# Attention: each pair's V products moved next to the scores that follow them, and the output projection moved into the banks of the q, k, v products

## What is computed

```python
h = _ln(x, ln1_g, ln1_b) + shift
qkv = (h @ Wqkv.T).reshape(b, n, 3, H, HD)
q = _ln(qkv[:, :, 0].transpose(0, 2, 1, 3), qn_g, qn_b)
k = _ln(qkv[:, :, 1].transpose(0, 2, 1, 3), kn_g, kn_b)
v = qkv[:, :, 2].transpose(0, 2, 1, 3)
scores = jnp.einsum('bhnd,bhmd->bhnm', q, k) / jnp.sqrt(jnp.float32(HD))
attn = jax.nn.softmax(scores, axis=-1)
o = jnp.einsum('bhnm,bhmd->bhnd', attn, v)
o = o.transpose(0, 2, 1, 3).reshape(b, n, H * HD)
x = x + o @ Wout.T
gate = jax.nn.softmax(tok @ Wgate.T, axis=-1)
```

## Time and profile before

| | |
|---|---|
| times of three runs | 1450.46, 1447.7, 1451.57 us |
| median | 1450.46 us |
| span of the profiled execution, first to last instruction | 1449.0 us |
| TensorE matmuls busy | 1391.5 us, 96% |
| TensorE weight loads | 1175.2 us, 81% |
| ScalarE | 1041.2 us, 72% |
| VectorE | 968.6 us, 67% |
| GpSimd | 913.1 us, 63% |
| mean granted TensorE clock | 0.986 of 2.4 GHz |

### The profile page before, as it was taken

One profiled execution on the slowest core, in us unless ns is written; L12 is line 12 of the kernel. 1 busy time (PEld: TensorE's weight loads), 2 busy tenths in 40 slices (PEclk: granted clock), 3 DMA queues, 4 the chain that ended last, 5 costly groups with the idle time before them and its releaser, 6 DMA issues. The chain is left out here.

```text
span 1449.0 us, 30428 instructions
## 1 busy us (share of the span) xinstructions
PE 1391.5 (96%) x10795; PEld 1175.2 (81%) x10795; DVE 968.6 (67%) x2250; ACT 1041.2 (72%) x2762; POOL 913.1 (63%) x855
## 2 busy tenths in 40 slices
PE   7899999997899999999999999999999989999997
PEld 6899999995677877787787778777787778889896
DVE  6877776645666676576667667667656568678763
ACT  5566666556898789888888888888988742466662
POOL 2676667643668767867776876876777620364633
PEclk9899999999999999999999999999999999999999
DMA  5432222110100100110110110011011127145522
GB/s 157 130 109 67 73 67 74 48 30 30 37 9 30 52 34 19 53 45 9 52 45 17 44 52 23 31 52 45 9 45 38 37 99 296 37 107 152 140 34 29
DMA packets 61638, 89.04 MB, mean 61 GB/s; under 512 B 6144, under 2 KB 50992, under 8 KB 58800
## 3 DMA queue, kind: packets, MB, share of 16 engines
q1 hardware_dynamic: 53232, 75.82, 16.1%
q0 software_dynamic: 6144, 8.39, 3.5%
q10 hardware_dynamic: 2112, 2.88, 0.6%
HBM read 61.90 MB, written 25.18 MB: 60 GB/s over the span
## 5 line engine op out<-in xcount | busy, mean ns | idle before, releaser
L1349 POOL TENSOR_TENSOR prob<-prob,share_p 128x512 f32<-128x512 f32 x256 | 271.8, 1069 | 214.3 <-DVE share_p L1456 214.3
L1450 DVE TENSOR_REDUCE shift<-bank 128x2 f32<-128x512 f32 x256 | 164.7, 684 | 235.2 <-PE bank L1083 235.2
L1230 ACT ACTIVATE prob<-bank,shift 128x256 f32<-128x256 f32 x512 | 236.8, 485 | 77.7 <-DVE shift L1450 77.6
L147 PE MATMUL bank<-wqkv_h,rowsT_h 128*128 128x512 f32 x384 | 159.5, 415 | 2.8 <-PEq L311 1.7
L147 PE MATMUL bank<-wqkv_h,rowsT_l 128*128 128x512 f32 x384 | 151.1, 394 | 0.0
L147 PE MATMUL bank<-wqkv_l,rowsT_h 128*128 128x512 f32 x384 | 151.0, 393 | 0.0
L1110 PE MATMUL bank<-pT,landing 128*64 128x256 f32 x1024 | 139.6, 394 | 4.4 <-ACT pT L1306 4.4
L1095 PE MATMUL bank<-ident,prob 128*128 128x128 f32 x1024 | 140.3, 280 | 0.5 <-POOL prob L1349 0.5
L1337 POOL TENSOR_TENSOR landing<-landing,rq 128x512 f32<-128x512 f32 x128 | 132.0, 1053 | 8.4 <-DVE rq L1404 8.4
L1095 PEld LDWEIGHTS bank<-ident,prob 128*128 128x128 f32 x1024 | 109.5, 141 | 18.6 <-POOL prob L1349 1.0
L1230 ACT ACTIVATION_READ_ACCUMULATOR prob<-bank,shift 128x1 f32 x512 | 110.9, 217 | 0.0
(11 more groups left out here) (324 smaller groups left out, 4557.4 us busy)
## 6 DMA issues: line engine op xcount, KB each, us to landing
landing<-in_fc1s SPq DMA_DIRECT2D x6, 1024.0 KB, 4.8
landing<-in_fc2s SPq DMA_DIRECT2D x6, 1024.0 KB, 4.8
rows<-in_x SPq DMA_DIRECT2D x16, 256.0 KB, 3.0
xT<-in_xT SPq DMA_DIRECT2D x16, 256.0 KB, 2.7
x_again<-in_x SPq DMA_DIRECT2D x16, 256.0 KB, 2.7
x_rows<-x SPq DMA_DIRECT2D x16, 256.0 KB, 3.2
rows<-x_rows SPq DMA_DIRECT2D x16, 256.0 KB, 3.1
x<-x_rows SPq DMA_DIRECT2D x16, 256.0 KB, 2.8
```

The lines of the kernel that those rows point to most:

```text
L147: last = nc.tensor.matmul(out, a, b, start=(n == 0), stop=(n == 3 * len(ks) - 1))
L1230: last = nc.scalar.activation(prob[at][:, n, :], score_bank[side][:, n * T:(n + 1) * T], ACT.Exp, bias=shift[:, at, n:n + 1], scale=-1.0, ...
L1349: nc.gpsimd.tensor_tensor(prob[at][:, :, :], prob[at][:, :, :], share[:, at, :].unsqueeze(2).to_broadcast([P, TT, T]), ALU.mult).then_inc( ...
L1450: nc.vector.tensor_reduce(shift[:, s % 2 * 2 + side, :], score_bank[side][:, :].rearrange("p (n m) -> p n m", n=TT), AX, ALU.min).then_inc ...
```

## The change

On TensorE the odd fill moves from behind the V products to before them, in all blocks but the closing one. So the order of a pair step becomes scores, transposes, even fill, chunks or projection, odd fill, V products, and the next pair's scores follow the V products directly. The projection of sequences 0 to 13 writes the chunk banks instead of `tr`; its two entries leave `TR_FILLS`, and it waits for the chunk that used the bank before (`chunk_out`), while chunks 8 and 9 wait for its copy (`out_proj`). For sequences 14 and 15 it stays where it was. On ScalarE, at the start of a pair step, the copy of the projection and the emptying of the odd fill now come before the taking of the V products; the copy of the projection thereby moves from the end of pairs 2 and 3 to the start of pairs 3 and 4. Where the even fill is emptied does not change.

```diff
-TR_FILLS = [("x2", 0, 1), ("h", 0, 2), ("gates", 0, 3), ("proj", 0, 4), ("qk", 0, 5), ("proj", 1, 6)] + [("qk", j, 6 + j) for j in range(1, 8)]
+TR_FILLS = [("x2", 0, 1), ("h", 0, 2), ("gates", 0, 3), ("qk", 0, 5)] + [("qk", j, 6 + j) for j in range(1, 8)]
+PROJ_PAIRS = 2, 3
...
+        def proj_bank(b, n):
+            return chunk_bank[n] if b < NB - 2 else tr
...
-                def project(t, b, n, its):
+                def project(b, n, its):
                     wait(pe, o_lo, PAIRS, b, PAIRS)
+                    if b < NB - 2:
+                        wait(pe, chunk_out, 12, b + 2, 7 + n)
+                    else:
+                        wait(pe, out_gates, 1, b - 1, 1)
+                        wait(pe, out_proj, TT, b, n)
...
-                    tr_free(pe, t, "proj", n)
-                    product(nc, tr[:, 0:D], ...
+                    product(nc, proj_bank(b, n)[:, 0:D], ...
...
                     wait(pe, chunk_out, 12, b, j - 1)
+                    if j in (8, 9):
+                        wait(pe, out_proj, TT, b - 2, j - 7)
...
                         for c, j in chunks_at(t, s):
                             if live(c):
                                 chunk(c, j)
-                        c, name, n = fill_at(t, 2 * s)
-                        if name == "proj" and live(c) and not closing(t):
-                            project(t, c, n, 1 - odd)
+                        if not closing(t):
+                            if s in PROJ_PAIRS and live(t - 1):
+                                project(t - 1, PROJ_PAIRS.index(s), 1 - odd)
+                            fill(t, 2 * s + 1)
                         for b, q, its in values_at(t, s, odd):
                             if live(b):
                                 values(b, q, its)
...
-                        fill(t, 2 * s + 1)
+                        if closing(t):
+                            fill(t, 2 * s + 1)
...
                     for s in range(PAIRS):
+                        if not closing(t) and not closing(t - 1):
+                            if s - 1 in PROJ_PAIRS and live(t - 1):
+                                projected(t - 1, PROJ_PAIRS.index(s - 1))
+                            empty(*fill_at(t, 2 * s - 1), 1 - odd)
                         for b, q, its in taken_at(t, s, odd):
...
-                        empty(*fill_at(t, 2 * s - 1), 1 - odd)
+                        if closing(t) or closing(t - 1):
+                            empty(*fill_at(t, 2 * s - 1), 1 - odd)
```

More of the change, by code:

```diff
@@ L863 @@
 LOW_PLACE = [(3,1),(4,1),(5,1),(5,1),(6,1),(6,1),(7,1),(7,1)]
-TR_LAG = {"h": 2, "proj": -1, "x2": -2, "gates": -2, "qk": 1}
-TR_PER = {"h": 1, "proj": TT, "x2": 1, "gates": 1, "qk": 8}
+TR_LAG = {"h": 2, "x2": -2, "gates": -2, "qk": 1}
+TR_PER = {"h": 1, "x2": 1, "gates": 1, "qk": 8}
 PAIRS = H // 2
@@ L982, in o_at, with late @@
             return q + 2 * its if q < 2 else q + 2
+        def late(b, q):
+            return (b, q) >= (NB - 2, PAIRS - 2)
         def values_bank(b, q):
-            return chunk_bank[1] if (b, q) >= (NB - 2, PAIRS - 2) and q % 2 == 0 else o_bank
+            return (chunk_bank[1] if late(b, q) and q % 2 == 0 else o_bank)[:, 0:T]
         def wait_x2(eng, b):
@@ L1004, in raw_block @@
             return raw[:, QK_ORDER[j], :].rearrange("p (m n) -> p m n", m=4)
-        drained = {"h": out_h, "proj": out_proj, "x2": out_x2, "gates": out_gates, "qk": out_qk}
+        drained = {"h": out_h, "x2": out_x2, "gates": out_gates, "qk": out_qk}
         def tr_free(eng, t, name, j):
@@ L1101, in values @@
                     wait(pe, pT_dve, PAIRS, b, q + 1)
-                    wait(pe, o_lo, PAIRS, b, q - 1 if (b, q) >= (NB - 2, PAIRS - 2) else q)
+                    wait(pe, o_lo, PAIRS, b, q - 1 if late(b, q) else q)
                     if (b, q) == (NB - 2, PAIRS - 2):
@@ L1109, in values @@
                             h = 2 * q + side
-                            last = nc.tensor.matmul(values_bank(b, q)[side * HD:(side + 1) * HD, 0:T], v[its][:, m, h * HD:(h + 1) * HD],
+                            last = nc.tensor.matmul(values_bank(b, q)[side * HD:(side + 1) * HD, :], v[its][:, m, h * HD:(h + 1) * HD],
                                                     pT[q % 2 * 2 + side][:, m, :], start=(m == 0), stop=(m == TT - 1))
                     last.then_inc(pv_done, 1)
-                def project(t, b, n, its):
+                def project(b, n, its):
                     wait(pe, o_lo, PAIRS, b, PAIRS)
+                    if b < NB - 2:
[3 more added lines that the diff above has]
+                        wait(pe, out_proj, TT, b, n)
                     if first(b):
                         pe.wait_ge(wo_lo, FIRST_LO + 4)
-                    tr_free(pe, t, "proj", n)
-                    product(nc, tr[:, 0:D], lambda k: (o_h[:, o_at(k, its), n * P:(n + 1) * P], o_l[:, o_at(k, its), n * P:(n + 1) * P]),
+                    product(nc, proj_bank(b, n)[:, 0:D], lambda k: (o_h[:, o_at(k, its), n * P:(n + 1) * P], o_l[:, o_at(k, its), n * P:(n + 1) * P]),
                             lambda k: (wo_h[:, k, :], wo_l[:, k, :]), range(HW // P)).then_inc(tr_proj, 1)
@@ L1147, in fill @@
                     b, name, j = fill_at(t, i)
-                    if name in (None, "proj") or not live(b) or name == "h" and first(b):
+                    if name is None or not live(b) or name == "h" and first(b):
                         return
@@ L1213, in step @@
                                 values(b, q, its)
-                        if name == "proj" and closing(t):
-                            project(t, c, n, 1 - odd)
+                        if closing(t) and s in PROJ_PAIRS:
+                            project(t - 1, PROJ_PAIRS.index(s), 1 - odd)
                         if closing(t) and s >= 4:
@@ L1255, in empty @@
                                              bias=cols[:, g + 1:g + 2], scale=cols[:, g:g + 1]).then_inc(out_qk, 1)
[L1256 to L1259, removed]
                     if name == "x2":
@@ L1265, in empty, with projected @@
                         nc.scalar.activation(logit[:, bass.ds(b * TT, TT), :], fill_bank(b)[:, 0:TT * E].rearrange("p (n e) -> p n e", n=TT), ACT.Copy).then_inc(out_gates, 1)
+                def projected(b, n):
+                    wait(act, tr_proj, TT, b, n + 1)
+                    wait(act, tr_gates, 1, b - 1, 1)
+                    nc.scalar.activation(proj[:, n, :], proj_bank(b, n)[:, 0:D], ACT.Copy).then_inc(out_proj, 1)
                 def chunk(b, j, odd):
@@ L1294, in step @@
                                     wait(act, tr_proj, TT, b - (2 if q == 0 else 1), TT)
-                                nc.scalar.activation(o_h[:, o_at(q, its), :], values_bank(b, q)[:, 0:T], ACT.Copy).then_inc(o_hi, 1)
-                        empty(*fill_at(t, 2 * s - 1), 1 - odd)
+                                nc.scalar.activation(o_h[:, o_at(q, its), :], values_bank(b, q), ACT.Copy).then_inc(o_hi, 1)
+                        if closing(t) or closing(t - 1):
+                            empty(*fill_at(t, 2 * s - 1), 1 - odd)
                         for n in range(TT):
@@ L1308, in step @@
                         high_parts(t, s, range(7 if late else 8), odd)
-                        if fill_at(t, 2 * s)[1] != "proj":
-                            empty(*fill_at(t, 2 * s), 1 - odd)
+                        empty(*fill_at(t, 2 * s), 1 - odd)
                         if late:
@@ L1315, in step @@
                                 chunk(c, j, odd)
-                        if fill_at(t, 2 * s)[1] == "proj":
-                            empty(*fill_at(t, 2 * s), 1 - odd)
+                        if closing(t) and s in PROJ_PAIRS:
+                            projected(t - 1, PROJ_PAIRS.index(s))
                         for q in range(4):
@@ L1468, in step @@
                                 wait(dve, o_hi, PAIRS, b, q + 1)
-                                nc.vector.tensor_tensor(o_l[:, o_at(q, its), :], values_bank(b, q)[:, 0:T], o_h[:, o_at(q, its), :].bitcast(F32), ALU.subtract).then_inc(o_lo, 1)
+                                nc.vector.tensor_tensor(o_l[:, o_at(q, its), :], values_bank(b, q), o_h[:, o_at(q, its), :].bitcast(F32), ALU.subtract).then_inc(o_lo, 1)
                         if closing(t - 1) and s == 3:
```

## The result

The changed kernel takes 1471.65 us (median of 4 runs, 1470.9 to 1472.53); the kernel before, measured beside it, 1450.68 us. The ratio is 1.0144, 95% interval 1.0131 to 1.0157: slower by 21.0 us, where 24.1 were forecast, and inside the stated range. The profiled execution took 1470.9 us with a span of 1469.1, so 1.8 us lie around it.

A forecast was written before the change was run, and what follows sets the result against it. Attention was taken as bound by TensorE's order and hand-overs. Waits in pairs 4 to 6 (17.6 + 12.3 = 29.9 us) less 5.8 saved gave +24.1 on 1450.46: 1474.5 us, range 1465 to 1482.

The forecast's parts named there:

- The mechanism: Pairs 4 to 6: the moved odd fill waits for ScalarE to empty the even fill from `tr`, delaying V products and scores.
- The waits of pairs 4, 5 and 6: Next scores start later by 0.35, 0.82 and 0.88 us a pair; the fill starts 0.14 us after the emptying's end.
- The saved hand-over: On TensorE, the new order's steps sum to 1.80 us against 1.91, saving 0.11 us per odd fill if nothing waits.
- The projection as the fill's neighbour: The projection's last matmul before the odd fill, in place of a chunk's: same 0.11 us saving assumed, bounds 0 and 0.2.
- Block 0: Pairs 2 and 3: the fill fits into TensorE's idle hole, saving 0.6 us each, 1.2 together; bounds 0 and 1.9.
- the other three items: Range bounds: 44 waits 2.2 us either way; hand-overs 4.5 worse, 3.7 better; block 0 1.2 worse, 1.9 better.
- the clock rival: Idle time in pairs 5 and 6 drops TensorE's clock to 0.77, 28 x 2.0 = 56 us more: 1530; chance 0.02.
- No wait, only the saved hand-over: ScalarE empties early enough, so the odd fills never wait: 12.0 us saved, 1438.5 us; chance 0.05.
- ScalarE did not fall behind: Rival: the late fill pushes ScalarE's exponentials, each of 44 pairs losing some 0.3 us more: 1488; chance 0.04.
- The wait was not smaller than worked out: Rival: ScalarE's chain is shorter or hand-overs save more, 0.3 us off each of 44 waits: 1461; chance 0.05.
- The projection costs nothing: Projection in the chunk banks: its wait for chunks 6 and 7 of pair 1 is covered by over 2.1 us.

The follow-up runs named there:

- the first experiment: The changed kernel, with ScalarE emptying the even fill before it makes the high parts: 1437.67 us, ratio 0.9913 against the kernel before.
- the still earlier emptying: The changed kernel, with the even fill emptied directly behind the exponentials, ahead of the pT copy and high parts: 1432.99 us, ratio 0.9883 against the kernel before.

## Why the prediction was right, and where its sizes were off

**The mechanism** held in each step. The odd fill waits for the emptying of the even fill of its pair (waits view of the changed kernel). The V products do not pass it (they start 0.56 us behind it in pair 5). The emptying's own time does not move with the fill: in pair 5 it ended 5.87 us after the scores both before and after. Take the wait away and the loss is gone; make it longer and the loss grows by about as much (8.6 us for 15 x 0.53 = 8.0); put it where there is cover and it costs nothing. The Trainium skill, "TensorE: Matmul & The Clock Gate", section Step-by-step, says that matmuls stay in program order. The trace agrees: the ready V products followed the waiting fill, 773.24 - 772.68 = 0.56 us behind it.

**The waits of pairs 4, 5 and 6** were worth +0.35, +0.82 and +0.88 a pair on record. By the pair lengths of block 7 (7.06, 7.58, 7.58 against 6.70, 6.76, 6.70) it was +0.36, +0.82 and +0.88. The 0.14 us from the emptying's end to the fill was met to 0.01.

**The saved hand-over was too small**, 0.11 where pairs 0, 2 and 3 of block 7 gained 0.16, 0.16 and 0.13 (6.14, 6.24 and 6.26 against 6.30, 6.40 and 6.39). The step that was mis-sized is fill to V products: I took 0.56 from a fill that had waited. A fill that has not waited hands over after 0.53 us, 0.52 to 0.54 in the pairs of blocks 2 to 13, as the first experiment's timeline shows for one (755.69 - 755.17 = 0.52). That is 0.03 of the 0.04 by which I was off; the last 0.01 is spread over the other steps. In pair 2 of block 7 of the changed kernel it was 0.54:

```profile
751.80 0.60 PE L1185 MATMUL bank<-ident,landing 128*128 128x128 f32 x4
752.34 1.08 PE L1119 MATMUL bank<-pT,landing 128*64 128x256 f32 x8
```

Over the 41 fills that is 41 x 0.04 = 1.6 of the 3.1 us by which the forecast was too high. The projection as the fill's neighbour lay inside its bounds of 0 and 0.2.

**Block 0** gave 2.5 us and not 1.2: pairs 2 and 3 last 5.22 us each where they had lasted 5.81 and 7.16. The upper bound came true there, since the clock of pair 3 stayed at 1.00; I had it only as a bound and could not say which it would be. That is another 1.3 us. The last 0.2 and some small terms of both signs (pair 1 costs 0.03 and not 0.02, block 14, pair 1 gains 0.18 and not 0.1) are below what the runs resolve.

**All pairs together.** From the first scores of block 0 to the last scores of block 15 the profiled execution took 805.10 us before (364.71 to 1169.81) and 826.60 after (364.26 to 1190.86), 21.5 more. Of these, pairs 4 and 5 make +17.7 and pair 6 +12.2, which is the forecast to 0.1. Pair 0 makes -2.1, pairs 2 and 3 make -4.1 and in block 0 another -2.5, and all the rest +0.3. So the cost was sized rightly, and the forecast was too high because the gains beside it were sized too small.

**Two slips in the forecast's numbers.** The 2 us that it lists for the runs' own spread are not in its bounds: 1467 and 1482 are 1474.5 with the other three items alone. And pairs 5 and 6 with idle time are 29, not 28, which would make the clock rival 1532. Neither decided anything.

**The rivals.** "No wait, only the saved hand-over" was put at 1438.5 us; the kernel in which the wait is removed took 1437.67. The Trainium skill, "TensorEngine Tiling (Array Packing)", section Key Properties, says that changing the tiling mode drains TensorE; with one change of array shape fewer, the pairs without a wait got 0.13 to 0.16 us shorter, so the trace points the same way. How much of that is the drain, no run here separates, and it was not what decided. The clock did not fall: 1.00 in the pairs with idle time and over blocks 2 to 13 as a whole. ScalarE did not fall behind: the exponentials of pair 5 began 1.73 us after the scores, where it was 1.74. The wait was not smaller than worked out. "The projection costs nothing" was tested alone and held.

## What to carry to other kernels

When work is moved on the engine that sets the time, ask what it was covering where it stood: look up when the engine on the other side finishes, and compare that with the new start, not the old one. A shared buffer that is emptied behind other work can be freed too late once its next user comes earlier. Then the move and the emptier's order have to be changed together: here the move alone lost 21 us, the emptier's order alone did nothing, and both together gained 13. An average busy share of 86% said nothing of this.

## What was not expected of the hardware

A group of matmuls that had to wait for a semaphore hands over more slowly to the next group than one that did not. Four transposes to the V products take 0.56 us in pairs 4 to 6 of the changed kernel (0.55 to 0.57 in its blocks 2 to 13) against 0.53 in the same pairs of the first experiment (0.52 to 0.54), and the eight matmuls of the gates 0.96 against 0.88. Nothing here shows why.

And in block 0 the clock depended on little. The forecast put the 0.77 of pair 3 down to the hole of pair 2, but the trace of the kernel before has a second hole, in pair 3 itself:

```profile
384.74 1.98 PE L1110 MATMUL bank<-pT,landing 128*64 128x256 f32 x8 [2.20 <-ACT pT L1306]
```

The granted clock was still 1.00 in the scores and transposes between the two holes. It fell to 0.50, the level of 1.2 GHz, only at the end of the second hole, at about 384.5 us, and was back at 1.00 soon after the first scores of pair 4. The V products of pair 3 took 1.90 us to the start of the fill, where those of pair 2 took 1.02. In the changed kernel both holes were shorter, 1.77 us each, and the clock stayed at 1.00. Here are the V products of pair 2 in the changed kernel:

```profile
378.48 1.08 PE L1119 MATMUL bank<-pT,landing 128*64 128x256 f32 x8 [1.77 <-ACT pT L1329]
```

The other traces mostly repeat this. Pair 3 of block 0 ran at 0.77 to 0.80 in all five profiled kernels with the old order in pairs 2 and 3, and at 1.00 in four of the five with the new one. The fifth is the kernel of the still earlier emptying: there TensorE waited 0.23 us in pair 1 and 1.77 in pair 2, and pair 3 ran at 0.70. So a hole of 1.77 us is no guarantee of the full clock, and the runs do not show what decides.
